# A graph network on one core: logits with the head innermost, and the mask's penalty on ScalarE

## What is computed

```python
def _gat_conv(x, src, dst, W, al, ar, b, act):
    z = (x @ W).reshape(N, H, F)
    el = jnp.sum(z * al, axis=-1)
    er = jnp.sum(z * ar, axis=-1)
    e = jax.nn.leaky_relu(el[src] + er[dst], 0.2)
    m = jax.ops.segment_max(e, dst, num_segments=N)
    ex = jnp.exp(e - m[dst])
    s = jax.ops.segment_sum(ex, dst, num_segments=N)
    alpha = ex / s[dst]
    msg = z[src] * alpha[..., None]
    out = jax.ops.segment_sum(msg, dst, num_segments=N) + b
    return act(out)
```

## Time and profile before

| | |
|---|---|
| three runs | 6763.08, 6788.65, 6792.3 us |
| median | 6788.65 us |
| profiled execution, span from first to last instruction | 6767.4 us |
| median less that span | 21.25 us |
| VectorE (DVE) busy | 4197.1 us, 62% |
| TensorE (PE) busy | 4241.0 us, 63% |
| GpSimd (POOL) busy | 3514.8 us, 52% |
| ScalarE (ACT) busy | 2122.3 us, 31% |

### The profile page before, as it was taken

How to read it: one execution, slowest core, us unless ns; L and a number is a source line. 1 busy time by engine, 2 the same in 40 slices (tenths; PEclk the granted TensorE clock), 3 DMA queues, 4 the chain that set the end, 5 groups by cost and what they waited for, 6 DMA issues and landing times.

```text
span 6767.4 us, 120783 instructions
## 1 busy us (share of the span) xinstructions
PE 4241.0 (63%) x28861; PEld 2819.0 (42%) x28861; DVE 4197.1 (62%) x13512; ACT 2122.3 (31%) x5941; POOL 3514.8 (52%) x4137
## 2 busy tenths in 40 slices
PE   1666666666566674544555555554778888888875
PEld 1333333333333352222322223222567776776764
DVE  4888888888888864777777777777731111224444
ACT  0555555555555532333333333333200000000000
POOL 4788888887777505777887777877000000000000
PEclk9777677777777786666666666666889999999998
DMA  5555555556555523555555555555389898999976
GB/s 96 159 166 161 163 168 157 164 155 172 164 157 166 159 76 90 143 142 135 143 147 141 145 146 143 143 146 141 86 360 416 330 415 335 415 416 400 366 317 274
DMA packets 913170, 1390.70 MB, mean 205 GB/s; under 512 B 481527, under 2 KB 661905, under 8 KB 896598
## 3 DMA queue, kind: packets, MB, share of 16 engines
q1 hardware_dynamic: 576475, 878.02, 37.0%
q0 software_dynamic: 128976, 222.12, 13.8%
q10 hardware_dynamic: 207462, 287.87, 12.3%
HBM read 1014.17 MB, written 373.27 MB: 205 GB/s over the span
## 4 chain that ended last, share of the span: by engine, by line
DVE 36%; DMA 18%; PE 13%; issue 13%; DVEq 11%; POOL 5%; SPq 4%; POOLq 0%; ACT 0%; ACTq 0%
DMA arena<-adj_w_d 9%; DVE arena L1051 7%; POOL arena L826 5%; DMA arena<-adj_c_d 4%; DVEq L1065 3%; DVE arena L1074 3%; DVE arena L1052 3%; PE bank L1842 3%; PE bank L1843 3%; PE bank L1846 3%; DVE arena L1186 2%; DVE arena L1081 2%; DMA arena<-msg_d 2%; DVE arena L1137 2%; DVE arena L1101 2%
## 5 line engine op out<-in xcount | busy, mean ns | idle before, releaser
L826 POOL DMA_INDIRECT arena<-table_d,arena x3136 | 3166.8, 1010 | 1159.3 <-issue 934.6
L1692 PE MATMUL bank<-arena 128*128 128x500 f16 x3750 | 1293.1, 499 | 1486.0 <-DVE arena L1137 1031.1
L1692 PEld LDWEIGHTS bank<-arena 128*128 128x128 f16 x3750 | 436.8, 125 | 2121.3 <-issue 1602.6
L1977 ACT ACTIVATE arena<-arena 128x128 f16<-128x128 f16 x3750 | 1126.1, 398 | 92.0 <-DVEq L1152 81.2
L1842 PE MATMUL bank<-arena 125*128 125x250 f16 x3750 | 862.3, 275 | 173.4 <-DMA arena<-adj_w_d 128.2
L1843 PE MATMUL bank<-arena 125*128 125x250 f16 x3750 | 858.3, 274 | 0.0
L1713 PE MATMUL bank<-arena 128*65 128x40 f32 x7500 | 582.8, 250 | 350.4 <-ACT arena L2020 328.4
L1051 DVE TENSOR_SCALAR arena<-arena 128x500 f16<-128x500 f16 x1875 | 703.6, 375 | 140.6 <-issue 124.6
L1713 PEld LDWEIGHTS bank<-arena 128*65 128x65 f32 x7500 | 567.1, 162 | 453.7 <-ACT arena L2045 436.3
L2045 ACT ACTIVATE arena<-arena 128x600 f32<-128x600 f32 x250 | 175.8, 703 | 1804.2 <-DVEq L1188 1804.2
L1694 PE MATMUL bank<-arena 128*128 128x500 f16 x1875 | 647.0, 464 | 0.0
(11 more groups left out here) (262 smaller groups left out, 4227.7 us busy)
## 6 DMA issues: line engine op xcount, KB each, us to landing
arena<-adj_w_d SPq DMA_DIRECT2D x720, 625.0 KB, 10.6
arena<-adj_c_d SPq DMA_DIRECT2D x345, 625.0 KB, 11.4
adj_w_d<-arena ACTq DMA_DIRECT2D x125, 1250.0 KB
arena<-msg_d SPq DMA_DIRECT2D x1250, 103.5 KB
msg_d<-arena POOLq DMA_DIRECT2D x196, 552.0 KB, 3.3
adj_c_d<-arena ACTq DMA_DIRECT2D x125, 625.0 KB
arena<-table_d,arena POOLq DMA_INDIRECT x3136
arena<-in_edge_features ACTq DMA_DIRECT2D x625, 51.0 KB
```

The source lines that it names most:

```text
L826: g_.indirect_dma_start(ring[:, i, k * XC:(k + 1) * XC], None, table_d, bass.IndirectOffsetOnAxis(ap=idx_cur[:, i, k:k + 1], axis=0)).then ...
L1692: mm(wb, lhsT=row_oh[:, slot, c, i, :], rhs=col_oh[:, slot, c, :], start=(c == 0 and i == 0), stop=(c == CH - 1 and i == 1))
L1977: last = act_(row_oh[:, slot, c, i, :], row_oh[:, slot, c, 2, :], ACT.Copy, scale=rec[:, c * REC + 2 + i:c * REC + 3 + i])
```

## The change

Seven things change, all in the two attention layers:

1. The logits `lg` lie as (window, chunk, node, head) in place of (window, chunk, head, node); the sum of source and destination parts is one instruction of 600 elements a partition in place of three of 200. The order of the aggregate's columns follows, in `finish` and in the code for overflowing windows.
2. The penalty is made by ScalarE (`penalties`, one ACTIVATE of 150 elements, at the head of a group's work), behind a new semaphore `keys_made`; VectorE's own instruction for it goes, and VectorE waits for `pen_made` before it adds it.
3. `top_p` and the first quarter of `top_r` share memory, so three small copies are made in place of four.
4. The drain after each window's one-hots goes; the last of them raises `onehot_made` itself.
5. `dve_step` is raised by the same 8 in a group, in three places (3 or 2, then 3, then the rest) in place of one by one.
6. SP masks the block count that it waits for with 127, one register operation a group.
7. The overflow code (windows with over 384 edges) follows; in the execution profiled it didn't run.

```diff
-        lg = new(P, WG, CH, H, WN)
+        lg = new(P, WG, CH, WN, H)
...
-        top_p = new(P, TQ)
-        top_r = new(BQ, P // BQ, TQ)
+        top_w = new(P, P // BQ, TQ)
+        top_p, top_r = top_w[:, 0], top_w[0:BQ]
...
-                    wait_reg(sp, s("msg_ready"), offs[WG] + layer * NBLK)
+                    wait_reg(sp, s("msg_ready"), (offs[WG] & 127) + layer * NBLK)
...
+        def keys_through(layer, g):
+
+            order = [x for h in range(NG) for x in keys_due(layer, h)]
+            return order.index(g) + 1
...
-        def paced(d, step):
-
-            drained = d.drain()
-            if step:
-                drained.then_inc(s("dve_step"), step)
-
-        def logits(d, par, rows, er, nw, step=0):
+        def logits(d, rows, er, nw, pens, extra_pens=None):
 
             n = nw * CH
-            e = er.rearrange("p (w j h) -> p w h j", j=WN, h=H)
-            for c in range(CH):
-                v.tensor_tensor(lg[:, 0:nw, c], bc(rows[:, :, c, F + 1:XC], 3, WN), e, ALU.add)
-            paced(d, step)
-            v.tensor_scalar(pen[:, 0:n, :], coh[:, par, 0:n, :], 1.0, BIG, ALU.subtract, ALU.mult)
-            z = lg[:, 0:nw].rearrange("p w c h j -> p (w c h j)")
+            e = er.rearrange("p (w j h) -> p w j h", j=WN, h=H)
+            v.tensor_tensor(lg[:, 0:nw], bc(rows[:, :, :, F + 1:XC], 3, WN), bc(e, 2, CH), ALU.add)
+            d.drain()
+            z = lg[:, 0:nw].rearrange("p w c j h -> p (w c j h)")
             v.scalar_tensor_tensor(z, z, 0.2, z, ALU.mult, ALU.max)
-            paced(d, step)
-            zz = lg[:, 0:nw].rearrange("p w c h j -> p (w c) h j")
-            v.tensor_tensor(zz, zz, bc(pen[:, 0:n, :], 2, H), ALU.add)
+            d.drain()
+            if pens is not None:
+                d.wait_ge(s("pen_made"), pens)
+            else:
+                d.wait_ge(s("ga_pen"), extra_pens)
+            zz = lg[:, 0:nw].rearrange("p w c j h -> p (w c) j h")
+            v.tensor_tensor(zz, zz, bc(pen[:, 0:n, :], 3, H), ALU.add)
             d.drain()
...
-            for q in range(P // BQ):
+            for q in range(1, P // BQ):
                 v.tensor_copy(top_r[:, q, :], top_p[q * BQ:(q + 1) * BQ, :])
...
                 for c in range(CH):
-                    one_hots(d, n % OHS, rec_sl[:, g, w, :], ckey[:, g, w * CH + c:w * CH + c + 1], c)
-                d.drain().then_inc(s("onehot_made"), 1)
+                    last = one_hots(d, n % OHS, rec_sl[:, g, w, :], ckey[:, g, w * CH + c:w * CH + c + 1], c)
+                last.then_inc(s("onehot_made"), 1)
...
-                        d.drain()
+                        d.drain().then_inc(s("keys_made"), 1)
                     for n in todo:
                         adjacency(b, n)
-                        d.sem_inc(s("dve_step"), 1)
+                    d.sem_inc(s("dve_step"), len(todo))
...
                     tops(d, top_b[:, par])
-                    paced(d, 1)
+                    d.drain().then_inc(s("dve_step"), 3)
...
+        def penalties(oh, out):
+
+            return act_(flat(out), flat(oh), ACT.Copy, scale=BIG, bias=-BIG)
...
-                act_(gst[:, g].rearrange("p h (w j) -> p w h j", j=WN), agg_sum.rearrange("p (w h j) -> p w h j", w=WG, h=H), ACT.Copy).then_inc(s("win_evac"), 1)
+                act_(gst[:, g], agg_sum.rearrange("p (n h) -> p h n", h=H), ACT.Copy).then_inc(s("win_evac"), 1)
...
                     todo = list(steps_of(layer, g))
+                    act.wait_ge(s("keys_made"), b * NG + (ng + keys_through(layer, g)))
+                    penalties(coh[:, g], pen).then_inc(s("pen_made"), 1)
                     for n in todo:
                         weigh(b, n)
```

More of the change, by code:

```diff
@@ L315, in build @@
             "wgat_loaded el_psum table_made table_stored er_stored "
-            "onehot_made rows_weighted adj_psum adj_evacuated seg_evacuated ov_loaded ov_onehot ov_weighted ov_psum ov_added "
-            "ov_stored logits_made exp_made win_psum win_evac "
+            "onehot_made keys_made pen_made rows_weighted adj_psum adj_evacuated seg_evacuated ov_loaded ov_onehot ov_weighted ov_psum ov_added "
+            "ov_stored logits_made exp_made win_psum ga_keys ga_pen win_evac "
             "ga_loaded ga_top ga_topt ga_diag ga_topp ga_logits ga_exp ga_psum ga_added "
@@ L1051, in one_hots @@
             v.tensor_scalar(col_oh[:, slot, c, :], iota_key, key, None, ALU.is_equal)
-            v.tensor_scalar(row_oh[:, slot, c, 2, :], iota_lo, rec[:, c * REC + 1:c * REC + 2], None, ALU.is_equal)
+            return v.tensor_scalar(row_oh[:, slot, c, 2, :], iota_lo, rec[:, c * REC + 1:c * REC + 2], None, ALU.is_equal)
         def keys(d, par, recs, wn, nw):
@@ L1176, in win_vector @@
                     d.wait_ge(rows_loaded[g], b * ROWS + ROWS * (layer * B + 1))
-                    logits(d, g, rows_sl[:, g], er_sl[:, g], WG, step=1)
+                    logits(d, rows_sl[:, g], er_sl[:, g], WG, b * NG + (ng + g + 1))
                     low_part(b, todo[-1] - 3)
@@ L1182, in win_vector @@
                     tops(d, top_b[:, par])
-                    paced(d, 1)
+                    d.drain().then_inc(s("dve_step"), 3)
                     wait_some(d, s("exp_made"), b * NG + (ng + former_group(g) + 1))
-                    v.tensor_tensor(gd[:, g % GS].rearrange("p (w c) k -> p w c k", c=CH), lg.rearrange("p w c h j -> p w c (h j)"),
+                    v.tensor_tensor(gd[:, g % GS].rearrange("p (w c) k -> p w c k", c=CH), lg.rearrange("p w c j h -> p w c (j h)"),
                                     bc(top_b[:, par, 0:WG * WH].rearrange("p (w k) -> p w k", k=WH), 2, CH), ALU.subtract)
@@ L1240, in win_overflow_vector @@
                     keys(d, 0, rec_sl[:, 0, 0:1], win_node[:, bass.ds(win, 1)], 1)
-                    d.drain()
-                    logits(d, 0, rows_sl[:, 0, 0:1], er_sl[:, 0, 0:WN * H], 1)
+                    d.drain().then_inc(s("ga_keys"), 1)
+                    logits(d, rows_sl[:, 0, 0:1], er_sl[:, 0, 0:WN * H], 1, None, kk + 1)
                     d.drain().then_inc(s("ga_top"), 1)
@@ L1250, in win_overflow_vector @@
                     v.tensor_tensor(top_o[:, 2, :], top_o[:, 0, :], top_o[:, 1, :], ALU.subtract)
-                    v.tensor_tensor(gd[:, 0, 0:CH, :], lg[:, 0].rearrange("p c h j -> p c (h j)"), bc(top_o[:, 1, :], 1, CH), ALU.subtract)
+                    v.tensor_tensor(gd[:, 0, 0:CH, :], lg[:, 0].rearrange("p c j h -> p c (j h)"), bc(top_o[:, 1, :], 1, CH), ALU.subtract)
                     d.drain().then_inc(s("ga_logits"), 1)
                     d.wait_ge(s("ga_exp"), kk + 1)
-                    v.tensor_tensor(ov_agg, ov_agg, top_o[0:AGG, 2, :], ALU.mult)
+                    sums = ov_agg.rearrange("p (h n) -> p n h", h=H)
+                    v.tensor_tensor(sums, sums, top_o[0:AGG, 2, :].rearrange("p (n h) -> p n h", h=H), ALU.mult)
                     d.drain()
                     d.wait_ge(s("ga_psum"), kk + 1)
-                    v.tensor_tensor(ov_agg, ov_agg, bank[6][0:AGG, 0:WH], ALU.add)
+                    v.tensor_tensor(sums, sums, bank[6][0:AGG, 0:WH].rearrange("p (n h) -> p n h", h=H), ALU.add)
                     d.drain().then_inc(s("ga_added"), 1)
@@ L2069, in win_overflow_scalar @@
                     kk = ga_base(act, layer) + k
+                    act.wait_ge(s("ga_keys"), kk + 1)
+                    penalties(coh[:, 0, 0:CH, :], pen[:, 0:CH, :]).then_inc(s("ga_pen"), 1)
                     act.wait_ge(s("ga_logits"), kk + 1)
```

2 lines of the change are left out of this document (1 added, 1 removed).

## The result

| | before | changed |
|---|---|---|
| median | 6788.62 us (6763.08 to 6792.3, 4 runs) | 6695.09 us (6691.03 to 6724.56, 4 runs) |
| profiled span | 6767.4 us | 6696.1 us |

The ratio of the times is 0.9886, 95% interval 0.9856 to 0.9915: **1.1% faster**. The forecast was 6700 us. Measured again later, with 13 runs of before and 4 of the changed kernel, the ratio was 0.9901 (0.9884 to 0.9917), 6762.46 us against 6696.81. The two profiled spans differ by 71.3 us.

The account below looks back on a forecast made before the run. VectorE was taken to bind layer 0, with POOL close behind, and POOL layer 1. Savings of 86 us in layer 0 and 3 in layer 1, contention 0, took the median from 6788.65 to 6700 us, range 6640 to 6765.

Parts of the forecast that it names:

- VectorE's 16.2 us a group: Layer 0: sums, penalty, copies and drains save VectorE 1.75 us a group, bounds about 0.2 and 2.0, from 17.96.
- The wait for `pen_made`: VectorE before adding the penalty: 0.1 us idle a group, bounds 0 and 0.2; longer waits would show the forecast wrong.
- An odd start of the rows of 69 floats: VectorE's sum: every second run starts on an odd word, adding at most 0.15 us.
- POOL then sets the end of layer 0: VectorE uses up POOL's lead in some 40 groups, then waits for rows; POOL needs 17.6 us a group.
- The saving of 86 us in layer 0: Layer 0 ends at 2335 us against 2420.8; bounds from POOL's pace 41 and 113 us saved.
- the contention: Other engines lengthening POOL's gathers: change taken as 0, bounds 22 us either way.
- POOL is slowed: Rival: the unbroken sum holds up one gather a group for 0.78 us, 195 us in all, giving 6895; chance 0.07.
- a mark of a wrong forecast: POOL's gathers averaging over 1.03 us would show the forecast wrong.
- The steps were put at 0: Later `dve_step` raises within a group cost nothing; they matter only where POOL is at its lead limit of 6 groups.
- Layer 1's gathers unchanged: POOL's 1568 gathers in layer 1 still take 2172 us, within 20; only the tail shrinks, by 3 us.
- The forecast of 89: Whole kernel: 86 us saved in layer 0 plus 3 in layer 1's tail.
- The rival of the late penalty: ScalarE reaches the penalty 3.5 us later than reckoned, or sum and drains save nothing: about 6770 us; chance 0.12.

Follow-up runs that it names:

- second set: Four variants of the changed kernel, one of them unaltered, on a chip like the first measurement's; there the kernel before took 6762.46 us, the changed kernel 6696.81.
- The spare reductions: Changed kernel with seven unused reductions, each with a drain, behind each group's tops on VectorE: 7091.08 us, ratio 1.0481 to the kernel before.
- the moved low part: Changed kernel with VectorE's last low part of a group ahead of the penalty's addition, and index lists copied once a block: 6728.82 us, ratio 0.9949 to before.

## Why the prediction was right, point by point

**VectorE's 16.2 us a group: right.** Between the subtractions of groups 0 and 12 of layer 0, while POOL's lead lasts, the changed kernel takes (388.30 - 193.4) / 12 = 16.24 us. By parts: the sum was to take 0.87 us and took 0.85; the windows' drains gave the 0.3 us each that was reckoned. Of the 0.63 us that the sum gave, 0.49 are the layout's. The wait for `pen_made` shows 0.17 us idle, between the 0.1 taken and the bound of 0.2. The copies gave 0.13 of the 0.2. An odd start of the rows of 69 floats shows no cost in a sum of 0.77 us, so the estimate of up to 0.15 us a group that was worked out from the Trainium skill (Vector Engine (DVE) Microarchitecture Reference, 5.2, Measured stream behaviour on trn2) is not borne out.

**POOL then sets the end of layer 0: right.** The lead (gathers ended at a group's subtraction, in groups of 12.54, less the groups taken) goes from 4.1 groups to 2.1 by group 24, and VectorE waits for `msg_d` from there. It is sooner than the 40 groups given because two groups of lead were there to lose, and not three; the end is 32.7 us behind the last gather, forecast 33.

**The saving of 86 us in layer 0 was 68.6, and the term mis-sized is the contention.** It was put at 0 within 22 us, and cost 17. The last gather ended at 2319.5 instead of 2302, one each 1.414 us in place of 1.403. The gathers alone would have cost more: they take 1038 ns in layer 0, and 1016 (796.33 / 784) in the early part of before, from which the pace came. 22 ns over 1498 gathers are 33 us. The copies of the index lists gave as much back, first before (200 to 1300 us), then now (200 to 2320 us):

```profile
L808 POOL COPY arena<-arena 128x4 int32 x196 | 63.1, 322 | 0.9
```

```profile
L813 POOL COPY arena<-arena 128x4 int32 (+1 forms) x374 | 87.2, 233 | 1.8
```

What stays are mostly POOL's stores, which stood 13.1 us waiting for gathers to land, in the early part of before 0.2. The prediction reckoned contention on the gathers alone. One meeting of the two engines, in order of time, POOL and VectorE:

```profile
1000.54 1.50 POOL L831 DMA_INDIRECT arena<-table_d,arena  x1 [0.31 <-issue]
```

```profile
1000.44 0.78 DVE L1082 TENSOR_TENSOR arena<-arena 128x600 f32<-128x600 f32 x1 [0.16 <-issue]
```

The gather starts 0.10 us into the addition and is 0.56 us longer than one of 0.94. By the Trainium skill (SBUF — State Buffer, "SBUF: two separate sides") whichever of the two starts first holds the shared ports for its whole length, and the 0.56 us lie near the 0.68 that the addition still had to run. Gathers of layer 0 that overlap this addition are 475 ns over 942 on average (123 of them), 288 before the change (140): 58 us in all in place of 40. Gathers of 1.4 to 1.6 us rose from 35 to 128 in layer 0, one a group. The new unbroken sum, which the rival "POOL is slowed" named, is not where it happened. Gathers that start in it are 13.6 us over 942 ns in all, where those that started in the three sums were 25.1. The rest of the rise is at the subtraction (2.5 to 14.8 us) and the one-hots of 128 (0.8 to 14.5). Such sums tell where the engines met, and not what slowed a gather. So that rival worked by another way than it gave, at 20 ns a gather, where it decides from 39. The mean over the program is 3231.3 / 3136 = 1030 ns, a hair over the 1.03 us that was named as a mark of a wrong forecast, and 1031 in the second measurement.

**The steps were put at 0: wrong by 27 us.** The prediction said that they matter only where POOL is at the limit of its lead. Given one at a time they save 27 us on the fast chip, 21 of them in layer 1, where the lead is some two groups.

**Layer 1's gathers unchanged: right, by things that cancel.** Gathers cost 27 us more, while the copies took 84.7 us in place of 97.5 and stores waited 0.3 us in place of 16.0.

**The median hit by more than the sum deserves.** The spans differ by 71.3 us and not 89; but the median of before lay 21 us above its span and the median of the changed kernel 1 us below its own. The second set's medians differ by 65.6 us. The forecast of 89 was too large by a fifth to a quarter of itself, inside its bounds. That the median came within 5 us of 6700 is in part luck.

**The rival of the late penalty** was given 0.12 for the reason that ScalarE's order is fixed. In the changed kernel on the fast chips its wait is 26.3 us in all, 8 times and only in layer 1, where VectorE waits for POOL anyway. A wait for `pen_made` was named as a sign of being wrong, and these are too few to be it. ScalarE was done 4.0 us ahead of the addition at the median of layer 0, where 3.5 were reckoned. (The terms named for VectorE's earlier coming add to 1.5 us and not 1.6.) The 3.5 us of slack from the earlier trace rows were real there and say nothing of a chip where TensorE, and ScalarE behind it, come 20 us late.

**The cap.** 125 groups by 1.75 us are 219 us of VectorE's time, and the layer gained 68.6. The spare reductions show the two regimes by themselves: 328.5 us in layer 0, 53.5 in layer 1. What beats both kernels on the fast chip is steps one at a time (6670.07 us, run). The lists once a block without the moved low part may do so too. Their 73 us in layer 1 were measured only together with it, and alone they were run only on a slow chip.

## What to carry to other kernels

When two engines bind different stages and are within 2% of each other, a saving on one is worth the distance to the other and the stored lead, whatever its size: cost the second engine's pace before counting instructions. Handing a cheap operation to an idle engine adds an order: it is free only as long as everything queued ahead of it there is punctual, so ask what the worst of that would cost. And compare variants on one chip, with the kernel before beside them, as a change that gains 1% on one can lose on the next: here 3.7%, with the lists copied once a block on both sides (7921.05 against 7638.10).

## What was not expected of the hardware

- Two of the three sets' chips ran the kernel before 12.6 to 13.0% slower, with VectorE and ScalarE as long busy as on the third and TensorE idle for nothing that the records show 1880 to 2170 us in place of 27. The extra time lies in the two attention layers. In one such stretch, of some 20 us, instructions came 0.70 or 1.40 us apart on TensorE and SP.
- Three sums of 200 elements took 504 ns each where one input was read with a stride, and 358 ns without; one sum of 600 takes 0.77 us.
- With fewer and larger index copies and one low part moved, gathers went from 1020 to 986 ns in layer 1. Which of the two edits did it was not told apart.
- An explicit drain with a semaphore between two one-hots costs 0.3 us that goes when the last one-hot raises the semaphore itself; alone it gave 1.7 and 2.3% on the slow chips.
